# Window attention with a routed MLP: scores in two 64x64 tiles, half of the expert and convolution products behind the attention product, and whole-tile transfers with their own slot for z

## What is computed

```python
x = x + conv_ref(ln_c(x), qkv_w, lepe_w, bias_table)
t = to_tokens(x)
t = t + ffn_ref(ln_t(t), router_w, router_b, expert_w, expert_b)

# conv_ref: for shift 0 and shift 2 (the image rolled by 2), for each half of 32 channels
qkv  = einsum('oi,bihw->bohw', qkv_w, xh)          # q, k, v of 32 channels each
lepe = depthwise 3x3 convolution of v
attn = softmax(q * scale @ k + bias)               # 4x4-pixel windows, 8 heads of 4
out  = attn @ v + lepe                             # summed over the two shifts
# ffn_ref: softmax router over 8 experts, top 2, weights normalised
y    = sum of 2 of 8 (64 x 64) expert products, weighted
```

## Time and profile before

| | us |
|---|---|
| median of 3 runs (lowest, highest) | 3488.29 (3474.26, 3489.13) |
| the profiled execution, its own time | 3467.97 |
| span of its profile | 3466.1 |
| PE busy | 3080.1 (89%) |
| DVE busy | 2229.3 (64%) |
| ACT busy | 1620.3 (47%) |
| POOL busy (DMA issue) | 2501.0 (72%) |
| mean granted clock of PE, share of full | 0.943 |

### The profile page before, as it was taken

The page is one execution under the profiler, slowest core; times in us unless marked ns, Lnnn a source line. Parts: engine busy times, 40 slices in busy tenths (PEclk is TensorE's granted clock), DMA queues, the critical chain, the costliest instruction groups (busy, mean ns, idle before and its releaser), DMA issues.

```text
span 3466.1 us, 202400 instructions
## 1 busy us (share of the span) xinstructions
PE 3080.1 (89%) x84772; PEld 1797.6 (52%) x84772; DVE 2229.3 (64%) x4807; ACT 1620.3 (47%) x3362; POOL 2501.0 (72%) x4998
## 2 busy tenths in 40 slices
PE   4899998989989898988889989989889999999996
PEld 2555555555555455554555545555455555555552
DVE  2566666666666666676666667666666666666675
ACT  2554444444444454444445444444444445454541
POOL 4887767767777677777767777777677777777760
PEclk7999999999999899999999999999999999999997
DMA  2456565555656565565556555555555565656555
GB/s 63 109 136 168 145 160 140 160 145 149 160 140 165 140 160 147 146 160 139 159 150 156 153 153 154 155 149 149 149 149 158 150 162 152 168 152 165 156 147 156
DMA packets 447180, 517.72 MB, mean 149 GB/s; under 512 B 120976, under 2 KB 415376, under 8 KB 446096
## 3 DMA queue, kind: packets, MB, share of 16 engines
q1 hardware_dynamic: 280336, 390.69, 41.4%
q0 software_dynamic: 165888, 113.57, 13.2%
HBM read 312.67 MB, written 77.86 MB: 113 GB/s over the span
## 4 chain that ended last, share of the span: by engine, by line
PE 64%; SPq 10%; issue 9%; DMA 9%; DVE 4%; ACT 4%; DVEq 0%; ACTq 0%
PE bank L622 15%; PE bank L707 11%; PE bank L687 10%; PE bank L607 7%; DMA z<-fin 3%; SPq L501 3%; PE bank L713 3%; PE bank L647 3%; PE bank L727 3%; PE bank L660 3%; SPq L531 3%; DMA gate_rows<-gateT 2%; PE bank L721 2%; PE bank L732 2%; PE bank L746 2%
## 5 line engine op out<-in xcount | busy, mean ns | idle before, releaser
L575 POOL DMA_DIRECT2D vx<-vt x3072 | 1555.6, 515 | 458.1 <-PE bank L713 446.1
L563 POOL DMA_DIRECT2D kx<-k_sb x1536 | 737.1, 488 | 419.0 <-issue 268.7
L707 PEld LDWEIGHTS bank<-probT,vx 128*32 128x32 f32 x36864 | 607.9, 150 | 438.2 <-issue 393.9
L622 PE MATMUL bank<-kx,qx 32*32 32x64 f32 x36864 | 705.3, 226 | 107.3 <-issue 79.9
L622 PEld LDWEIGHTS bank<-kx,qx 32*32 32x32 f32 x36864 | 597.5, 111 | 387.8 <-issue 374.2
L707 PE MATMUL bank<-probT,vx 128*32 128x16 f32 x36864 | 672.2, 210 | 139.7 <-issue 126.8
L939 DVE TENSOR_TENSOR gx<-gate_wide,yn_pair 128x768 f32<-128x768 f32 x384 | 365.6, 953 | 463.3 <-DMA gate_wide<-gate_rows 293.6
L796 ACT ACTIVATE prob<-prob 128x512 f32<-128x512 f32 x576 | 360.3, 626 | 267.1 <-DVE prob L951 253.4
L687 PE MATMUL bank<-halo,conv_w 128*64 128x380 f32 (+6 forms) x2592 | 460.3, 482 | 1.1 <-issue 1.1
L951 DVE TENSOR_TENSOR prob<-bank,row_max 128x512 f32<-128x512 f32 x576 | 398.5, 692 | 16.7
L946 DVE TENSOR_REDUCE row_max<-bank 128x32 f32<-128x512 f32 x576 | 382.7, 664 | 38.1 <-PE bank L622 30.0
(11 more groups left out here) (72 smaller groups left out, 2969.7 us busy)
## 6 DMA issues: line engine op xcount, KB each, us to landing
gate_wide<-gate_rows SPq DMA_DIRECT2D x768, 192.0 KB
vx<-vt POOLq DMA_DIRECT2D x3072, 12.0 KB
halo<-xn SPq DMA_DIRECT2D x160, 240.0 KB
kx<-k_sb POOLq DMA_DIRECT2D x1536, 24.0 KB
z<-fin SPq DMA_DIRECT2D x192, 192.0 KB, 5.7
yn_pair<-yn POOLq DMA_DIRECT2D x384, 96.0 KB
xa<-in_x SPq DMA_DIRECT2D x192, 96.0 KB, 4.3
xn<-xa SPq DMA_DIRECT2D x192, 96.0 KB
```

The source lines that it names most:

```text
L563: pool.dma_start(kx[to + m:to + C:4, r % 2, m, :], k_sb[at + m:at + C:4, r % 2, :])\
L575: pool.dma_start(vx[to:to + TOK, r % 2, col:col + 13:4, odd, :], vt[at:at + TOK, r % 2, x::2, :, :].rearrange("p h n k -> p h (n k)"))\
L622: last = MM(bank_s[r % 2][at, w * KEYS:(w + 1) * KEYS], qx[at, kr % 2, win, :, :].rearrange("p a i -> p (a i)"), kx[at, kr % 2, :, win * T ...
L707: last = MM(bank_o[32 * c:32 * c + 32, at * TOK:(at + 1) * TOK], vx[:, kr % 2, :, at % 2, at // 2 * 4 + ba], probT[:, kr % 2, at, ba * TOK ...
```

## The change

- **Scores.** A window's scores are made by two products with 64x64 tiles (one for each shift) where there were four with 32x32. The query gets 4 column blocks in place of 2, so ACT makes 4 masked copies of it (Q_PARTS) where it made 2, in each slot 0 and 3. Tables (`mask_q`, `ones`, the order of heads, the bias) and the columns of vx follow. A score unit is 16 products instead of 32.
- **Order on PE.** Experts of place 1 and the convolution's sides 1 and 2 stand behind the attention product; side 0 stays ahead of it. Pair 3 goes from place 0 to place 1 of slot 2.
- **Order on DVE.** The tile's output (`tile_out`) goes to the end of the slot's body.
- **Transfers.** x, its reordered copy and the output lie in HBM as 128-row tiles, so each takes one DMA where it took two. The halves of z are read with one DMA each; the rolled z takes 2 (3 at an image's start) where it took 6. The z loads stand in `load_z` at lag 35 and have a semaphore of their own; the wait for z's stores goes with them, and `y_second` waits for the loads. A tile has 27 DMAs on SP where it had 34.

```diff
-    store_z=24, load_halo=29, load_tile=33, conv=34, ...
+    store_z=24, load_halo=29, load_tile=33, load_z=35, conv=34, ...
-EXPERT_AT = {(0, 0): 0, (1, 0): 1, (1, 1): 2, (2, 0): 3}
+EXPERT_AT = {(0, 0): 0, (1, 0): 1, (1, 1): 2, (2, 1): 3}
...
-        "mask_q": ((p[:, None] // 16 & 1) == np.arange(2)[None, :]) * HD ** -0.5,
+        "mask_q": ((p[:, None] // 16 & 3) == np.arange(4)[None, :]) * HD ** -0.5,
...
-        qx = sb("qx", [128, 2, WIN, 2, TOK])
+        qx = sb("qx", [128, 2, WIN, 4, TOK])
...
-                for half in range(2):
-                    at = (r % IMT * (2 * SP) + half * SP) * W
-                    sp.dma_start(xa[half * C:(half + 1) * C, r % 2, :],
-                                 x_flat[bass.ds(im, 1)][:, :, at:at + SPX].rearrange("b c n -> c (b n)"))\
-                        .then_inc(x_loaded[r % 2], 16)
+                sp.dma_start(xa[:, r % 2, :], whole(x, bass.ds(im, 1), r % IMT)).then_inc(x_loaded[r % 2], 16)
...
                 if ti := s.tile("load_tile"):
                     k, r = ti
+                    if s.later(r, 2):
+                        wait_alone(sp, y_made, k - 1)
+                    sp.dma_start(xt[:, r % 2, :], whole(x_tile, bass.ds(s.image(r, IMT), 1), (r + 1) % IMT))\
+                        .then_inc(xt_loaded[r % 2], 16)
+                if ti := s.tile("load_z"):
+                    k, r = ti
...
                     for p in range(2):
                         wait_alone(sp, z_stored[p], counts[p] * 16)
...
-                    for half in range(2):
-                        put_x(half)
-                        put_z(z0t, half, 0, 0, 0, 4, 0, t * (2 * SP) + half * SP, SP)
...
+                    for half in range(2):
+                        sp.dma_start(z0t[half * C:(half + 1) * C, r % 2, :], part(z_of[0], im, (t * 2 + half) * SPX))\
+                            .then_inc(z_loaded[r % 2], 16)
...
-                        for g in range(4):
-                            at = slice(g * CH, g * CH + CH)
+                        for half in range(2):
+                            at = slice(half * C, half * C + C)
                             last = MM(bank_s[r % 2][at, w * KEYS:(w + 1) * KEYS],
                                       qx[at, kr % 2, win, :, :].rearrange("p a i -> p (a i)"),
                                       kx[at, kr % 2, :, win * TOK:(win + 1) * TOK],
                                       start=False, stop=(w == UW - 1), skip_group_check=True)
...
-                expert(1)
...
+                conv((0,))
                 if u := s.unit("product"):
...
                     last.then_inc(pv_made, 1)
+                expert(1)
+                conv((1, 2))
...
-                    for a in range(2):
+                    for a in range(Q_PARTS):
                         S.activation(qx[:, r % 2, :, a, :].rearrange("p n (r w) -> p n r w", w=SP),
                                      windows(bank_p[0][:, 0:SPX]), ACT.Copy,
                                      scale=const("mask_q")[:, a:a + 1]).then_inc(q_saved, 1)
...
-                if yt := s.tile("tile_out"):
...
                 gate_work((10, 12), (0, 0))
+                if yt := s.tile("tile_out"):
+                    k, r = yt
+                    dve.wait_ge(expert_made, (k + 1) * PAIRS)
...
+                    V.tensor_tensor(y_out[:, r % 2, :], bank_f[:, 0:SPX], y[:, r % 4, :], ALU.add).then_inc(y_out_made, 1)
```

More of the change, by code:

```diff
@@ L220, in lay_tables @@
             for m in range(HEADS):
-                a, b, y = m // 4, m // 2 % 2, m % 2
+                at = (m + 2 * roll) % HEADS
+                a, b, y = at // 4, at // 2 % 2, at % 2
                 for part, name in ((0, "wq"), (1, "wk")):
-                    put(name, rows, g * CH + a * 16 + h * 4 + m % 4, qkv_w[part * CH + h * HEADS + m])
-                here = (h - 1) % HD if roll and a and b else h
+                    put(name, rows, g * CH + a * 16 + h * 4 + at % 4, qkv_w[part * CH + h * HEADS + m])
+                here = (h - 1) % HD if roll and at < 2 else h
                 put("wv", rows, g * CH + h * 8 + y * 4 + b * 2 + a, qkv_w[2 * CH + here * HEADS + m])
@@ new lines, in put_rolled @@
+                    def put_rolled(half, at, row, rows):
+                        sp.dma_start(z2t[half * C:(half + 1) * C, r % 2, at * W:(at + rows) * W],
+                                     z_of[1][im][:, :, row * W:(row + rows) * W].rearrange("b c n -> c (b n)"))\
+                            .then_inc(z_loaded[r % 2], 16)
+                    if t == 0:
+                        put_rolled(0, 0, H - ROLL, ROLL)
+                        put_rolled(0, ROLL, 0, SP - ROLL)
+                    else:
+                        put_rolled(0, 0, t * (2 * SP) - ROLL, SP)
@@ L609, in expert, with conv @@
                     last.then_inc(expert_made, 1)
+                def conv(sides):
+                    ti = s.in_tile("conv")
+                    if not ti or ti[2] not in sides:
+                        return
+                    k, r, side = ti
+                    t, dw = (r + 1) % IMT, SIDES[side]
+                    if side == 0:
+                        pe.wait_ge(halo_loaded[r % 2], halos_to(s, r) * 16)
+                        if s.later(r, 1):
+                            pe.wait_ge(y_step, k * 2 - 1)
+                    low, high = max(0, -dw), W - max(0, dw)
+                    first = [side == 0, side == 0]
+                    for group, skip in ((0, 0), (1, 2)):
+                        parts = [(half, *rows) for half in range(2) for rows in conv_rows(t, half)[group]]
+                        for half, top, end, which in sorted(parts, key=lambda part: part[1]):
+                            at = half * SP + skip
+                            last = MM(by_rows(bank_c[half * C:(half + 1) * C, 0:SPX])[:, top:end, low:high],
+                                      conv_w[:, which, group * 3 + side, :],
+                                      by_rows(halo[:, r % 2, :])[:, at + top:at + end, low + dw:high + dw],
+                                      start=first[half], stop=(side == 2 and group == 1), skip_group_check=True)
+                            first[half] = False
+                    if side == 2:
+                        last.then_inc(conv_made, 1)
                 if u := s.unit("score"):
```

102 lines of the change are left out of this document (35 added, 67 removed).

## The result

| | before | after |
|---|---|---|
| median of 4 runs each, side by side, us | 3486.93 (3474.26 to 3489.13) | 3448.62 (3445.78 to 3454.47) |
| ratio of after to before, 95% interval | | 0.9907 (0.9888 to 0.9925) |
| span and time of the profiled execution, us | 3466.1, 3467.97 | 3452.7, 3454.47 |
| mean granted clock of TensorE | 0.943 | 0.935 |

The change makes the kernel 38 us faster, 0.93%. The kernel before was profiled in an execution 20 us under its median, that of after in one 6 us over, so the two traces differ by 13 us only.

What follows compares the result with a forecast made beforehand. The prediction saw the kernel near PE's own work, with instruction stops and a slot 3 hole awaiting the key copy. Terms +52 - 73 - 20 + 19 + 24 = +2 us; put on the median, 3490 us, range 3395 to 3590.

Steps and rivals of the forecast that it cites:

- R1: Rival theory made after the result: the gain is the new order of experts and output, and the scores are neutral.
- T: Theory after the result: query copies lengthen the chain, fewer PE instructions bring the gain, the key copy sets the pace.
- (a): Chain through slots 2 and 3 to `tile_sum`: two more query copies, less the reordering, lengthen it 0.54 us a tile, +52 us.
- (b): PE's stops for instructions: fewer score instructions remove four fifths of 91 us; stops inside the chain give nothing; -73 us.
- (c): SP's queue: fewer DMAs and no wait for z's stores, so gates and halo come on time; -20 us.
- (e): PE's clock after the hole: 0.2 more half-clock stretches a tile, each worth 1.3 us; +24 us.
- (d): Scores on PE: 64-column loads under 64-column streams cost 0.04 us a unit, in five of six units; +19 us.
- (f): Slot 0: `centre` waits for all query copies, covered by 0.4 us; 0.5 us a tile if that cover is gone.
- The one that has starvation as the pace: Rival: all 91 us of PE's stops return, loads fit, the clock falls no more often; 3406 us, chance 0.32.
- fetches are late because of traffic and not rate: Rival: DMA traffic delays PE's code, so fewer instructions give 0 and the longer chain stays; 3563 us, chance 0.14.
- A hole that costs twice: Rival: a hole touching two stretches lowers PE's clock in both; 3615 us, or 3553 with half the tiles; chance 0.10.
- a distance of 9.2 us or less: Sign of a wrong forecast: slot 2's scores to `tile_sum` in 9.2 us or less would mean a kernel faster than forecast.

Runs made afterwards that it cites:

- e8: Changed kernel with experts, convolution and DVE's output back in their old order; 3487.5 us, ratio 1.0060 to the kernel before.
- e3: Changed kernel with 32x32 scores, old tables, two query copies and two more copies nobody reads; 3483.9 us, ratio 1.0050 to the kernel before.
- e2: Changed kernel with scores back in 32x32 tiles, two query copies and old tables; 3373.1 us, ratio 0.9727 to the kernel before.
- e9: Changed kernel without its scores: 32x32 tiles, two query copies, tables of the new order; 3385.4 us, ratio 0.9746 to the kernel before.
- e1: Kernel before with the 64x64 scores alone, order and transfers old; 3510.4 us, ratio 1.0082 to the kernel before.
- e5: Kernel before with the key copy ahead of its two query copies; 3471.1 us, ratio 0.9975 to the kernel before.
- e10: Changed kernel with 32x32 scores, two query copies, new tables, and the key copy first; 3303.0 us, ratio 0.9504 to the kernel before.
- e11: Changed kernel with DVE's output one slot later and the key copy first in slot 3 only; 3099.6 us, ratio 0.8906 to the kernel before.
- e4: Changed kernel with the key copy ahead of the four query copies; 3158.6 us, ratio 0.9094 to the kernel before.

## Why the prediction was wrong

R1 and T both hold a part: the order is worth 39 to 53 us (e8), fewer instructions 35 to 50 us (e3), and the two copies cost more than both together (e2 to e3, 111 us). The parts do not add up, since they cover each other: order and transfers gain 2.5% without the 64x64 scores (e9) and leave 0.9% with them (after).

**(a) The chain: right.** The least chain grew by 0.42 us (forecast 0.54), and nearly every tile waits for the key copy, 92 of 96, for 2.46 us on average. The miss is that the order gives 0.52 and not 0.39 us (e8), with 0.95 for the copies (e1; forecast 0.93).

**(b) Instructions: the step that failed.** It said of the stops in slot 3: "Those fall inside the chain of (a), which is as long without them, so they give nothing." They did not give nothing. In 56 of the 70 tiles a stop of over 0.8 us lies within the chain, and in 30 the chain is longer by more than 0.15 us, 0.41 us on the mean of all: a stop in slot 3's scores is on the chain, since the row maximum waits for them, and a stop of 2 us and more in the product outlasts the hole. Without stops this comes back: 0.40 us in 96 tiles, by estimate 38 us, as much as the whole change gained. It is the fewer instructions that bring it: the mean is 0.09 us over the least in e1, with the new scores alone, and 0.37 us in e9, with all but them. The forecast took the chain from one undisturbed tile, and so compared two least chains (+52 us) where the means count (+2 us). The removal of stops itself was understated too: 187 of 207 us are gone, not half; the 40 us left for the start and the loop's returns were too many, since after has 20 us in all.

**Outside the chain** the sum had -73 for the rest of (b), -20, +19 and +24, together -50; the rest fell by 0.32 us a tile, 31 us. Of that, (c) by PE's waits for gates is -14 us; (e) is 0.59 us more at half clock in a tile at 0.46 each (below), +26 us, close to the forecast.

**(d) is near the forecast too.** At full clock a score group in 64x64 tiles takes 1.078 us from its start to that of the next line, and one in 32x32 tiles 1.026, at the same place and with the same line behind it: so before against e1 and e8, and so e9 against after. What follows the group comes later by that, and does not make it good. That is 0.052 us a unit, where the forecast had 0.04, and five units a tile give an estimate of 25 us. The group of slot 2 shows it in e8, in its shortest rest (24.19 us), and in the shortest of before without half clock (24.42 us):

```profile
2518.29 1.15 PE L656 MATMUL bank<-kx,qx 64*64 64x64 f32 x32
2519.36 0.87 PE L617 MATMUL bank<-gx,table 128*64 128x384 f32 x4
```

```profile
2788.08 0.52 PE L622 MATMUL bank<-kx,qx 32*32 32x64 f32 x21
2788.81 0.86 PE L622 MATMUL bank<-kx,qx 32*32 32x64 f32 x43 [0.20 <-issue]
2789.59 0.87 PE L607 MATMUL bank<-gx,table 128*64 128x384 f32 x4
```

The rests seem to say that the load is free. But this group of before is stopped, and lasts 1.51 us in place of 1.03, of which only 0.20 us show as idle; without the stop its rest would be 23.94 us, 0.25 less than e8's, which is five groups' worth. The profile has a load at 147 ns in the mean against 111, which says little: the distance grew by 3 ns a load. The Trainium skill (TensorE: Matmul & The Clock Gate, LDWEIGHTS) had 53 ns and a term of 0 for it, and the trace differs from the 0 by those 3 ns. By difference some 68 us are left for (b) outside the chain, close to the 73.

**(f) Slot 0: right.** 7.0 us of waiting in 4 tiles.

Together: +2 in place of +52, and -31 in place of -50, make -29 us where the sum had +2; by the medians it is 38, by the two traces 13. So the step that decides is the one in the chain, 50 us.

**The rivals.** The one that has starvation as the pace, 3406 us, was right that fewer instructions pay more than was put down, and wrong in that the hole and the clock still take a good part. It missed by about as much. That fetches are late because of traffic and not rate is refuted by e1, which has the old transfers and 50.8 us of stops in place of 206.7; the new transfers in their place make it 45.4 (e8). A hole that costs twice does not show: half clock went from 3.56 to 4.15 us a tile, about one stretch each. Of what was to show it, one threshold was badly put: a distance of 9.2 us or less from slot 2's scores never came in any of the 70 tiles, and the kernel is faster nevertheless, because the bound was on the least and not the mean.

## What to carry to other kernels

A wait hides a stall only as far as it is longer in every instance: take a chain's length as the mean over all tiles, not from a tidy one, and compare it with the least; the difference is what disturbances add. When two bounds lie close together, an edit is worth little alone (9 us in e5) and much once the other is gone (82 us from e9 to e10, with the same two copies), so try the cheap reordering again after each change. Before work is added to an engine, look at which of its instructions has the impatient reader, and put that first.

## What was not expected

**Lack of code comes and goes with few instructions, and not by their pace alone.** By "issue" ahead of product and scores, the runs with 544 pieces of code stop for 19.6 us (after), 45.4 (e8) and 50.8 (e1), and in e11, whose tiles take 31 us in place of 34.5, for 30 us:

```profile
PE bank L656 <- issue: 19.4, 6, 4.2
...
PE bank L721 <- issue: 11.0, 25, 1.7
```

Those with 688 pieces stop for 104 us (e3), 133 (e2), 144 (e9), 168 (e10), 207 (before) and 239 (e5). e3 and before fetch the same pieces in the same time, 3484.0 and 3466.1 us, and differ by a factor of two: in e3 order and transfers are new and the wait for the key copy is 173 us, not 40. No run tells these apart. "Issue" understates the stops, as the group above under (d) shows. From one stop of over 0.5 us to the next, PE of before has a multiple of 256 instructions, its register and waiting ones counted in, within 20 in 122 of 136 cases, in keeping with a piece of 256 instructions. The Trainium skill (Advanced Engine Details and Errata, ISA Cache) gives that size too.

**The half clock costs nearly half of its length.** In e8, whose tiles differ in nothing else, the rest takes 24.19 us in a tile without it and 25.58 in one with 3.02 us of it: 0.46 us each, where the forecast had 1.3 us in 3.4. A hole of 2.5 us on PE brings one such stretch in every tile of after; in e4, with chains of 6.6 us and waits of 0.6 us on average ahead of `tile_sum`, the half clock is down to 0.39 us a tile.
